# An attention and mixture-of-experts layer on one core: the order of work in a head pair, and the first expert in two halves

## The reference, cut to what matters

```python
B, N, D = (16, 256, 256); H, HD = (16, 64); E, DD = (8, 1024)
shift = silu(t) @ W_ada.T + b_ada
h = _ln(x, ln1_g, ln1_b) + shift
qkv = (h @ Wqkv.T).reshape(b, n, 3, H, HD)
q = _ln(q); k = _ln(k)
attn = softmax(q @ k.T / sqrt(HD))
x = x + (attn @ v) @ Wout.T
gate = softmax(tok @ Wgate.T)
vals, idx = top_k(gate.T, 512)
g = _ln(tok[idx])
y = gelu(g @ fc1.T + b1) @ fc2.T + b2
tok = tok.at[idx].add(y * w)
```

## Time and profile before

| what | value |
|---|---|
| median of 3 runs | 1220.6 us (1219.45 to 1220.81) |
| the profiled execution | 1221.37 us, span 1219.6 us |
| PE busy | 1066.5 us, 87% of the span |
| DVE busy | 966.5 us, 79% |
| ACT busy | 714.6 us, 59% |
| POOL busy | 624.5 us, 51% |
| granted TensorE clock, mean | 0.96 of full speed |
| PE in a step, start to start where nothing waits | `mx` 0.79 to 0.87, `pq` 0.44, four transposes of rows or tokens 0.44, chunk 1.5 to 1.6, half a projection 1.5 to 1.6, `av` 1.0, `sc` 0.9, gates 0.9 |
| DVE, start to start | `probT` 1.14, `qkT` 0.43, `m` 1.13, `o_lo` 0.33, `ssum` 0.59 |
| ACT, start to start | one exponential 0.45, `qkT` 0.45, `V` 0.48, `o_hi` 0.28, `qk_hi` 0.52 |
| chain that ended last | PE 52%, DVE 30%, issue 12%, ACT 4%, DMA 1% |

### The profile page before, as it was taken

One profiled execution on the slowest core, in us unless ns is written; L12 is line 12 of the kernel. 1 busy time (PEld: TensorE's weight loads), 2 busy tenths in 40 slices (PEclk: granted clock), 3 DMA queues, 4 the chain that ended last, 5 costly groups with the idle time before them and its releaser, 6 DMA issues.

```text
span 1219.6 us, 24072 instructions
## 1 busy us (share of the span) xinstructions
PE 1066.5 (87%) x7843; PEld 855.6 (70%) x7843; DVE 966.5 (79%) x1696; ACT 714.6 (59%) x1970; POOL 624.5 (51%) x532
## 2 busy tenths in 40 slices
PE   7799999999999999999999999999984036999996
PEld 6577777777777777777777777777763035988995
DVE  4788888888888888888888888888875894777773
ACT  4667676766666676767666666767661103545541
POOL 2565556566556565556665565655561003355333
PEclk9999999999999999999999999999997557999999
DMA  4000000000001000000000010000002303355412
GB/s 172 18 9 19 19 19 18 17 17 17 17 17 33 11 25 17 17 17 17 17 17 17 17 34 12 23 9 19 10 18 103 101 1 123 104 171 137 108 22 31
DMA packets 31773, 48.59 MB, mean 40 GB/s; under 512 B 7920, under 2 KB 28528, under 8 KB 30448
## 3 DMA queue, kind: packets, MB, share of 16 engines
q1 hardware_dynamic: 25584, 39.49, 10.0%
q0 software_dynamic: 6144, 8.52, 3.8%
HBM read 35.29 MB, written 12.71 MB: 39 GB/s over the span
## 4 chain that ended last, share of the span: by engine, by line
PE 52%; DVE 30%; issue 12%; ACT 4%; DMA 1%; DVEq 1%; POOL 0%; SPq 0%; ACTq 0%
PE ch L488 8%; PE av L1482 7%; PE ch L489 7%; PE ch L490 7%; PE sc L1400 6%; DVE m L1287 5%; DVE qn L867 4%; PE mx L1450 4%; DVE probT L1243 4%; DVE ssum L1216 2%; PE pq L1437 2%; ACT prob L1104 2%; DVE o_lo L1292 2%; DVE xh L1171 2%; DVE bn L1157 2%
## 5 line engine op out<-in xcount | busy, mean ns | idle before, releaser
L961 POOL TENSOR_TENSOR prob<-prob,inverse 128x1024 f32<-128x1024 f32 x128 | 248.8, 1944 | 279.2 <-DVE inverse L1248 279.2
L1104 ACT ACTIVATE prob<-sc,m 128x256 f32<-128x256 f32 x512 | 235.6, 472 | 152.3 <-DVE m L1287 152.3
L1243 DVE COPY probT<-mx 128x1024 f32<-128x1024 f32 x128 | 156.4, 1222 | 82.4 <-PE mx L1450 81.3
L977 POOL TENSOR_TENSOR qk_lo<-qkT,qk_hi 128x512 fp32r<-128x512 f32 x128 | 171.8, 1342 | 36.2 <-ACT qk_hi L1092 32.4
L1287 DVE TENSOR_REDUCE m<-sc 128x4 f32<-128x1024 f32 x128 | 156.3, 1221 | 42.7 <-PE sc L1400 41.6
L488 PE MATMUL ch<-w_hi,hT_lo 128*128 128x512 f32 x384 | 170.4, 444 | 9.6 <-DVE hT_lo L1188 8.8
L1482 PE MATMUL av<-probT,V 128*64 128x256 f32 x1024 | 139.7, 394 | 22.6 <-DVE probT L1243 18.8
L490 PE MATMUL ch<-w_hi,hT_hi 128*128 128x512 f32 x384 | 152.2, 396 | 0.0
L489 PE MATMUL ch<-w_lo,hT_hi 128*128 128x512 f32 x384 | 152.1, 396 | 0.0
L1450 PE MATMUL mx<-con,prob 128*128 128x128 f32 x1024 | 133.6, 274 | 1.8 <-POOL prob L961 1.6
L1482 PEld LDWEIGHTS av<-probT,V 128*64 128x64 f32 x1024 | 62.4, 136 | 83.5 <-DVE probT L1243 55.4
(11 more groups left out here) (196 smaller groups left out, 2653.5 us busy)
## 6 DMA issues: line engine op xcount, KB each, us to landing
fcw<-experts SPq DMA_DIRECT2D x8, 2048.0 KB, 9.1
x_sb<-x SPq DMA_DIRECT2D x16, 256.0 KB, 2.7
xr_sb<-x SPq DMA_DIRECT2D x16, 256.0 KB, 2.8
out<-tok SPq DMA_DIRECT2D x16, 256.0 KB, 2.2
rows_dram<-xh SPq DMA_DIRECT2D x16, 256.0 KB, 2.2
prob<-w_qk SPq DMA_DIRECT2D x2, 512.0 KB, 7.2
qn<-w_qk SPq DMA_DIRECT2D x2, 512.0 KB, 8.6
V<-w_vT SPq DMA_DIRECT2D x2, 512.0 KB, 8.1
```

What stands on the lines that cost most here:

```text
L961: nc.gpsimd.tensor_tensor(pr, pr, r, ALU.mult).then_inc(normalised, 1)
L977: nc.gpsimd.tensor_tensor(qk_lo[par][:, :], qkT[par][:, :], qk_hi[par][:, :].bitcast(F32), ALU.subtract).then_inc(lo_ready, 1)
L1104: ins = nc.scalar.activation(prob[hp % 2][:, g * N:(g + 1) * N], sc[:, g * N:(g + 1) * N], ACT.Exp, bias=m[hp % 2][:, g:g + 1], scale=-1.0 ...
L1243: nc.vector.tensor_copy(probT[:, :], mx[:, :]).then_inc(probT_ready, 1)
```

## The change

It has four parts.

1. PE, in every step: the transposes to `mx` now stand ahead of those to `pq`. In the steps 3 to 7 of round 15, which have no chunks, the scores also stand ahead of `av`.
2. ACT, steps 1 and 5: the second V chunk is read in the step in which PE makes it, ahead of its exponentials.
3. DVE, steps 2, 6 and 7: the reciprocal stands behind `qn` (2 and 6), behind `xr_sb` and `xh` (7), just ahead of the maximum. At step 2 the split of the rows stands ahead of `o_lo`. In round -1 `qn` is taken at step 5, ahead of the low parts of the weights.
4. First expert: its tokens are transposed and split in two halves of 256, into banks that are free there, and the first four blocks of `fc1` run on the first half, then on the second. ACT loads its table for the gelu ahead of the tokens.

```diff
@@ ACT, round @@
-                    if (hp - 1, 1) in CHUNKS and (cur if hp <= 2 else nxt):
+                    if hp in (1, 4, 5) and (cur if hp <= 2 else nxt):
                         chunk(b, hp - 1, 1)
...
+                    if live and values:
+                        chunk(b, hp, 1)
                     if cur:
                         need(max_ready, u + 1)
@@ DVE, round @@
-                    if (cur and hp > 0) or (hp == 0 and prv):
-
-                        need(prob_ready, u)
-                        need(normalised, u - 2)
-                        nc.vector.reciprocal(inverse[(hp - 1) % 2][:, :], row_sum[(hp - 1) % 2][:, :]).then_inc(inverse_ready, 1)
+                    rows_first = hp in (2, 6, 7)
+                    if not rows_first:
+                        inverses(b, hp, cur, prv)
...
-                    if hp == 6 and nxt:
+                    if hp == 6 and nxt and not entry:
                         normalise(b, 4)
...
+                    if rows_first:
+                        inverses(b, hp, cur, prv)
                     if cur:
...
+                    if hp == 2 and nxt and not entry:
+                        split_rows(b)
                     if (cur and hp > 1) or (hp < 2 and prv):
...
-                    if hp == 2 and nxt and not entry:
-                        split_rows(b)
...
                     if entry and hp == 5:
+                        normalise(b, 4)
                         low_parts(1, 0)
@@ POOL, round @@
-                    if hp == 6 and nxt:
+                    if hp == (5 if isinstance(b, int) and b < 0 else 6) and nxt:
                         scale(b, 4, 3)
@@ PE, round @@
-                    if ahead:
-
-                        gpar, i = ((hp + 1) // GU) % 2, (hp + 1) % GU
...
-                        for c, at in ((0, 0), (2, 1), (1, 2), (3, 3)):
-                            ins = nc.tensor.transpose(pq[:, at * P:(at + 1) * P], qn[gpar][:, c, i * P:(i + 1) * P], ident)
-                        ins.then_inc(qk_transposed, 1)
                     behind = (cur and hp > 1) or (hp < 2 and prv)
                     if behind:
...
                                     ins = nc.tensor.transpose(mx[:, to:to + P], pr[:, at:at + P], ident)
                         ins.then_inc(prob_transposed, 1)
+                    if ahead:
+
+                        gpar, i = ((hp + 1) // GU) % 2, (hp + 1) % GU
...
+                        for c, at in ((0, 0), (2, 1), (1, 2), (3, 3)):
+                            ins = nc.tensor.transpose(pq[:, at * P:(at + 1) * P], qn[gpar][:, c, i * P:(i + 1) * P], ident)
+                        ins.then_inc(qk_transposed, 1)
                     if live:
                         chunk(b, hp, 0)
...
+                    filled = nxt or hp < 3
+                    if cur and not filled:
+                        scores(u, hp % 2)
                     if behind:
...
-                    if cur:
+                    if cur and filled:
                         scores(u, hp % 2)
@@ first expert @@
+        HALF = CAP // 2
+        first_tokens = ((sc[:, 0:HALF], sc[:, 512:512 + HALF]), (av[:, 0:HALF], pq[:, 0:HALF]))
+        first_fc1 = (ch[0], ch[1], mx[:, 0:CAP], mx[:, CAP:2 * CAP])
...
+            nc.scalar.preload_act_table_set("gelu_apprx_tanh_and_others")
+            for h in range(2):
+                half = slice(h * HALF, (h + 1) * HALF)
+                act.wait_ge(first_transposed, h + 1)
+                nc.scalar.activation(gT[:, 0, half], first_tokens[h][0], ACT.Identity,
+                                     bias=vec[:, MLP_B:MLP_B + 1], scale=vec[:, MLP_G:MLP_G + 1]).then_inc(first_full, 1)
...
+                V_.tensor_tensor(gT_lo[:, 0, half], gT[:, 0, half], gT_hi[:, 0, half].bitcast(F32), ALU.subtract).then_inc(first_lo_ready, 1)
...
+                if first:
+                    for h in range(2):
+                        half = slice(h * HALF, (h + 1) * HALF)
+                        pe.wait_ge(first_lo_ready, h + 1)
+                        for hc in range(4):
+                            for c in range(DC):
+                                cols = slice(hc * P, (hc + 1) * P)
+                                ins = three_passes(fc1_bank(e, hc)[:, half], w1_hi[:, c, cols], w1_lo[:, c, cols],
+                                                   gT_hi[:, c, half], gT_lo[:, c, half], c == 0, c == DC - 1)
```

More of the change, by code:

```diff
@@ L444, in build @@
         first_full = sem("first_full")
+        first_lo_ready = sem("first_lo_ready")
         first_other_full = sem("first_other_full")
@@ L605, in tokens @@
                 act.wait_ge(g_transposed, e)
-                act.wait_ge(gT_lo_ready, e)
+                if isinstance(e, int) and e == 1:
+                    act.wait_ge(first_lo_ready, 2)
+                else:
+                    act.wait_ge(gT_lo_ready, e - 1)
                 for dst in (gT_hi, gT):
@@ L670, in phase23_tensor @@
             ins.then_inc(lists_spread, 1)
-            for k in range(KT):
-                pe.wait_ge(first_gathered[k], 16)
-                for c in range(DC):
-                    ins = nc.tensor.transpose(ch[c][:, k * P:(k + 1) * P], got[0][:, k, c * P:(c + 1) * P], ident)
-            ins.then_inc(first_transposed, 1)
+            for h in range(2):
+                for k in range(2):
+                    pe.wait_ge(first_gathered[2 * h + k], 16)
+                    for c in range(DC):
+                        ins = nc.tensor.transpose(first_tokens[h][c][:, k * P:(k + 1) * P], got[0][:, 2 * h + k, c * P:(c + 1) * P], ident)
+                ins.then_inc(first_transposed, 1)
             def expert(e, pair, par):
@@ L679, in expert @@
                 w_lo_wait(pe, 1, e)
-                if not (isinstance(e, int) and e == 0):
+                first = isinstance(e, int) and e == 0
+                if first:
+                    for h in range(2):
+                        half = slice(h * HALF, (h + 1) * HALF)
+                        pe.wait_ge(first_lo_ready, h + 1)
+                        for hc in range(4):
+                            for c in range(DC):
+                                cols = slice(hc * P, (hc + 1) * P)
+                                ins = three_passes(fc1_bank(e, hc)[:, half], w1_hi[:, c, cols], w1_lo[:, c, cols],
+                                                   gT_hi[:, c, half], gT_lo[:, c, half], c == 0, c == DC - 1)
+                            if h == 1:
+                                ins.then_inc(fc1_done, 1)
+                else:
                     pe.wait_ge(gT_ready, e)
-                pe.wait_ge(gT_lo_ready, e + 1)
-                for hc in range(HC):
-                    if not (isinstance(e, int) and e == 0 and hc < 2):
-                        pe.wait_ge(gelu_done, e * HC + hc - 1)
+                    pe.wait_ge(gT_lo_ready, e)
+                for hc in range(4 if first else 0, HC):
+                    pe.wait_ge(gelu_done, hc - 3 if first and hc < 6 else e * HC + hc - 1)
                     for c in range(DC):
@@ L819, in low_part @@
                 V_.tensor_tensor(lo, full, hi.bitcast(F32), ALU.subtract).then_inc(ready, 1)
[L821 to L829 removed]
+            for h in range(2):
+                half = slice(h * HALF, (h + 1) * HALF)
+                dve.wait_ge(first_transposed, h + 1)
+                V_.tensor_scalar(gT[:, 1, half], first_tokens[h][1], vec[:, MLP_G + 1:MLP_G + 2], vec[:, MLP_B + 1:MLP_B + 2],
+                                 ALU.mult, ALU.add).then_inc(first_other_full, 1)
+                dve.wait_ge(first_other_full, h + 1)
+                V_.tensor_copy(gT_hi[:, 1, half], gT[:, 1, half]).then_inc(first_other_hi, 1)
+                dve.wait_ge(first_other_hi, h + 1)
+                V_.tensor_tensor(gT_lo[:, 1, half], gT[:, 1, half], gT_hi[:, 1, half].bitcast(F32), ALU.subtract)
+                dve.wait_ge(first_hi_ready, h + 1)
+                V_.tensor_tensor(gT_lo[:, 0, half], gT[:, 0, half], gT_hi[:, 0, half].bitcast(F32), ALU.subtract).then_inc(first_lo_ready, 1)
             def expert(e, pair, par):
@@ L1223, in _, with inverses @@
             input_rows(rstd[1])
+            def inverses(b, hp, cur, prv):
+                if (cur and hp > 0) or (hp == 0 and prv):
+                    u = b * UNITS + hp
+                    need(prob_ready, u)
+                    need(normalised, u - 2)
+                    nc.vector.reciprocal(inverse[(hp - 1) % 2][:, :], row_sum[(hp - 1) % 2][:, :]).then_inc(inverse_ready, 1)
             def flat_rows(t):
```

26 lines of the change are left out of this document (8 added, 18 removed).

## The result

The changed kernel takes **1187.8 us** (median of 4 runs, 1181.8 to 1189.3) against 1220.5 us of the kernel before beside it: a ratio of 0.972, with a 95% interval of 0.969 to 0.976. Run once more beside other kernels it took 1184.5 us (5 runs, 0.970, 0.968 to 0.972). The forecast was 1185. The profiled execution took 1186.44 us, its span is 1184.7 us.

A forecast was written before the change was run, and what follows sets the result against it. PE's own work was taken to set the pace. Gains of 28.8 (14 rounds) + 1.4 + 1.1 + 1.65 + 2.6 = 35.6 us took the span from 1219.6 to 1184.0, median forecast 1185 us, range 1169 to 1202.

The forecast's parts named there:

- step 6: PE's wait at step 6 for ACT's read of V goes: +1.04 us a round.
- step 7: DVE's two `xh` of the step before run beside POOL's pair, so `av` here is late: -0.25 us a round.
- step 0: `probT` is in time, +0.55 us a round; the late reciprocal delays POOL's product for PE, -0.30.
- step 2: PE's wait at step 2 for ACT's read of V goes: +1.13 us a round.
- step 3: PE's wait for `hT_lo` (0.79 us) stays within 0.1, `hT_lo` being done 2.0 us into the step as before.
- rival 3: POOL wins the turns; the split of the rows costs 2.1 us at step 3 every round: 1213 us, chance 0.08.
- The new order of the transposes: PE's transposes give `probT` 0.44 us earlier and `pq` 0.87 later; neither on the path, counted at nothing.
- V read earlier: ACT reads V 0.2 us into steps 2 and 6, so both waits of PE go: gain 1.04 + 1.13 us.
- both are ready: With V read earlier, `av` (3.0 to 3.4 us) finds `probT` done at 2.2; scores (about 4) find exponentials at 2.5.
- Rival 4: Slower: `qn`, ahead of the reciprocal, still takes 2.8 to 3.6 us, delaying POOL and PE: 1233 us, chance 0.04.
- Ends of the attention: Gains: rounds -1 and 0, 0.4 and 1.0 us; round 14 into 15, 1.1; last steps of round 15, 1.65.
- First expert: With tokens in halves PE starts `fc1` about 1.95 us earlier; with the table load 2.6 us, bounds 1.0 and 3.5.

The follow-up runs named there:

- run 4: The changed kernel with the transposes to `pq` ahead of those to `mx` again: 1197.6 us (0.979), a round of 54.29 us.
- D: DVE's new order (later reciprocals; at step 2 the split of the rows ahead of `o_lo`); alone on the kernel before: 1216.9 us (0.997).
- run 1: The kernel before with only the second chunk of V read ahead of the exponentials: 1209.2 us (0.992), a round of 54.97 us.
- run 3: The changed kernel with DVE's old order back (reciprocal first at every step): 1212.5 us (0.993), a round of 55.03 us.
- run 8: The changed kernel with the scores of round 15 behind `av` again at steps 3 to 7: 1186.0 us (0.971).
- run 7: The changed kernel with DVE's old order in round 15, at steps 2, 6 and 7: 1189.7 us (0.974).
- Run 9: The changed kernel; at step 7 of round 15 pair 6's reciprocal goes ahead of probT, residual and token rows a step later: 1181.9 us (0.969).
- run 11: Run 9's kernel with the two `xh` on the input rows at step 6 moved ahead of the reciprocal: 1177.1 us (0.965).
- run 12: The changed kernel once more, unchanged, beside run 11: 1184.5 us (0.970).
- run 10: The changed kernel with 28 unread identity transposes on PE while it waits for the first gathered tokens: 1187.9 us (0.972).

## Why the prediction was right, and where its steps were not

**Right for the changed kernel as a whole.** By steps, forecast against measured: step 6 +1.04 (the wait for V), measured 1.15; step 7 -0.25, measured -0.50; step 0 +0.55 - 0.30, measured 0.49, with the foreseen wait of 0.24 for POOL's product at 304.16; step 2 +1.13, measured 0.91; step 3 "stays within 0.1", measured 0.19. The sum was 2.06 with the small ends, measured 2.24. No term of a round is off by more than 0.25 us. The pair qn at 1.2 us (1.28), its neighbour xh held up at step 6 (2.50), hT_lo done 2.0 us into step 3 (1.7) and the absence of a table load among the gelus came as forecast. The turns between DVE and POOL hold; what has changed is which of their operations meet. That also answers the question to the Trainium skill (SBUF — State Buffer, section "SBUF: two separate sides"), which leaves open who gets the shared ports when both wait: at 323.13 to 325.3 DVE's two operations and POOL's qn and qk_lo start by turns, and each waits for one of the other's. With POOL winning always, rival 3, the split would have been 2.1 us later; it was not.

**Wrong in whom it credits.** "The new order of the transposes ... counts nothing" is false. It holds 0.72 us a round, 10 of the 35 us (run 4). The step that failed is "neither is on the path": I asked who waits for `pq` and for `probT`, and not what the transposes to `pq` themselves wait for. In the changed kernel D puts POOL's qn behind its product, and with `pq` first PE waits 1.35 us for it. And "V read earlier ... gain 1.04 + 1.13" is the result of three parts together; V alone gives 0.84 (run 1). The check "both are ready" looked at `av` and the scores of the same step, and not at `pq` and the chunk of step 3: in run 1 they wait for DVE's `qn` and `hT_lo` and take back all that step 2 had gained. Rival 4 had the mechanism, a long qn ahead of what PE needs: without D it takes 1.5 of the 2.24 us (run 3), though it never turns the sign. The sum was right because the times of the steps were worked out with all parts in place; a part by itself could not be read from it.

**Ends of the attention.** Behind step 2 of round 0 and up to step 3 of round 15 the forecast was 1.0 + 28.8 + 1.1 = 30.9 us, measured 31.8 (1.9 + 29.1 + 0.76). Round 0 was sized too high and the looped rounds too low: 0.3 us came before step 7 of round 0, where 1.0 was forecast, and 2.24 instead of 2.06 in a looped round. For the end of round 15 it was 1.65: "0.55 per pair, 2.2 in all, give back 0.5". Measured from step 3 to the last transposes of probabilities: 33.37 us against 32.74 before, a loss of 0.6, the same within 0.02 in four profiles of this code. Both terms were mis-sized. The scores in front, put at 2.2, give 0.4 up to step 7, since the exponentials of the pair before are late next, and over the whole stretch lose 0.5, since PE's clock falls a pair sooner (run 8). The later reciprocals cost 0.8 from step 7 on instead of 0.5 (runs 3 and 7), partly through the same clock, so the two do not add up: with the scores behind av and the reciprocals late the stretch is 32.89 us, 0.15 more than before. And the new order of the transposes, put at nothing, makes the stretch from step 3 on 1.3 us longer (run 4); how was not traced. At step 7 the exponentials of pair 6 end at 881.3, its reciprocal stands behind probT, residual and token rows until 884.34, and the maximum of pair 7 behind that. Run 9, which moves that work behind and this reciprocal even ahead of probT, gains 3.0 us up to the last transposes (30.31 against 33.35); it shows what the place of the work is worth there, more than the change had cost.

**First expert.** 2.6 forecast, 2.0 measured in this pair of profiles and about 1.6 over all. PE starts 1.79 us sooner behind the first transpose (3.04 against 4.83; forecast 1.95). The clock's rise does not always follow: in the profile of after it is at its upper level about 6 us behind the first transpose, in others of the same code 5.5 to 8.4 us, and the stretch is then up to 1.2 us longer.

**By luck.** That the gain between the two profiles, 35.0 us, comes so near to the 35.6 of the forecast is in part luck. Too much was forecast for the end of round 15 (by 2.7), the second row of the table (1.2) and the first expert (0.6); too little for the 13 rounds (2.3). The search gave 1.3 us though no part of the change touches it, and the first stretch 0.97, of which 0.4 was forecast; both lie within the spread of the same code.

## What to carry to other kernels

When several waits stand in a row on the engine that bounds a kernel, ask of each removed wait what is late next in the kernel with that edit alone and in the kernel with all edits: here half of the gain of a round existed only with three edits together, and one counted at nothing carried 10 us. Ask it in both directions, of what waits for the moved work and of what the moved work waits for. Work from SBUF to SBUF on DVE that is held up beside POOL (here `qn`, `xh`, `hT_hi`, `hT_lo`) belongs where POOL is idle, which is just ahead of the result that POOL waits for, as long as POOL's product has room behind it. Where the filler work ends, as in a last round, a rule made for the full rounds has to be taken back: the chain through the last items goes first.

## What the runs showed of the hardware

**Turns by whole instructions.** The same DVE operation on the same data takes 0.68 us or 1.76 us (qn, means), 0.41 or 1.29 us (xh on the input rows, means of runs 11 and 12), by what POOL does beside it, and POOL's product 1.90 or up to 2.45 us. Nothing of this is seen for operations that read PSUM (probT 1.22 us beside POOL and alone), nor for every one that reads SBUF: `ssum`, a reduction from SBUF to SBUF, takes 0.68 us beside POOL (66 times) and alone (38 times) in the changed kernel.

**The granted clock decides what is left of small gains.** PE's clock is at 2.4 GHz from round 0 to step 7 of round 15 and falls in the last pairs, where PE waits 2.21 us for POOL's product. The same code had it at 1.2 GHz from 886 through the last projection in one profile, and up again at 893 to 894, before it, in three others. Windows of the changed kernel, and of the run of the same code with the first expert in one piece (length, busy times, then PEclk before the last two):

```profile
888.00:893.00 5.00, 3.60 (x17) 1.99 (x16) 1.73 (x3) 0.39 (x1) 1.90 (x1) 0.50 0.00 0
893.00:898.00 5.00, 3.69 (x16) 2.16 (x16) 1.63 (x2) 0.39 (x1) 0.00 (x0) 0.50 0.00 0
```

```profile
889.00:894.00 5.00, 3.60 (x17) 2.00 (x16) 1.73 (x3) 0.38 (x1) 1.89 (x1) 0.50 0.00 0
894.00:899.00 5.00, 3.69 (x30) 2.92 (x29) 1.65 (x2) 0.38 (x1) 0.00 (x0) 0.99 0.00 0
```

PE is busy for the same time in both, and does 30 matmuls instead of 16 in the last window. It is worth 2.3 us from the last transposes to the tokens (10.29 against 8.02), with nothing in the program to choose it. Run 9, in which the clock stays up to that point, has neither loss.

**A warm clock can be lost again.** In run 10 the identity transposes brought the upper level before the first expert, and it fell again in the next idle time of 3.49 us.
